# Cross-attention and routed experts: two of the transposes into the row maxima's banks, rank counts behind the output projection, place computation one step later

## The reference, cut to what matters

```python
x = x + tanh(g_xattn[0]) * xattn(layernorm(x), ctx, Wq, Wk, Wv, Wo, bo)   # 8 blocks of 512 rows, 512 wide
x = x + tanh(g_ffn[0])   * ffn(layernorm(x), gate_w, Wu, Wv, Wo)          # each row goes to 2 of 8 experts

def xattn(x, context):                      # 8 heads of 64
    q, k, v = x @ Wq, context @ Wk, context @ Wv
    attn = softmax(q @ k.T / 8)             # per head, 512 x 512
    return (attn @ v) @ Wo + bo

def ffn(x):
    logits = x @ gate_w
    w = softmax(top_k(logits, 2))
    return sum of the two chosen experts' (silu(x @ Wu_e) * (x @ Wv_e)) @ Wo_e, weighted by w
```

## Time and profile before

| | |
|---|---|
| median of 3 runs | 1075.7 us (1075.69 to 1076.78) |
| the profiled execution | 1087.6 us |
| its span on the core | 1085.8 us |
| PE busy in the span | 897.2 us (83%) |
| DVE, ACT, POOL busy | 677.4, 571.8, 538.8 us |

### The profile page before, as it was taken

The page is one execution under the profiler, slowest core; times in us unless marked ns, Lnnn a source line. Parts: engine busy times, 40 slices in busy tenths (PEclk is TensorE's granted clock), DMA queues, the critical chain, the costliest instruction groups (busy, mean ns, idle before and its releaser), DMA issues.

```text
span 1085.8 us, 22768 instructions
## 1 busy us (share of the span) xinstructions
PE 897.2 (83%) x8210; PEld 544.0 (50%) x8210; DVE 677.4 (62%) x1595; ACT 571.8 (53%) x1022; POOL 538.8 (50%) x645
## 2 busy tenths in 40 slices
PE   4878988998899898899899989987540999799880
PEld 2334544555455455455455545544320787577660
DVE  5587876677777766867767786685334454344440
ACT  3366756566557555655755655556120564455450
POOL 6222253343565366546446645547563246556564
PEclk9998999999999999999999999999765899899995
DMA  7447634645633443364354225644343589889996
GB/s 266 132 135 243 215 117 119 170 113 112 191 100 73 133 127 103 75 176 112 75 154 141 68 62 188 185 119 125 110 140 113 142 186 196 167 177 205 189 154 85
DMA packets 125998, 154.53 MB, mean 142 GB/s; under 512 B 48448, under 2 KB 81216, under 8 KB 125120
## 3 DMA queue, kind: packets, MB, share of 16 engines
q1 hardware_dynamic: 102112, 103.08, 33.8%
q0 software_dynamic: 16864, 37.40, 17.8%
q10 hardware_dynamic: 6912, 12.59, 3.8%
HBM read 67.06 MB, written 56.56 MB: 114 GB/s over the span
## 4 chain that ended last, share of the span: by engine, by line
PE 54%; DMA 12%; DVE 12%; issue 8%; ACT 8%; POOL 3%; SPq 1%; POOLq 1%; ACTq 0%; DVEq 0%
PE G L1256 28%; DMA out_dram<-V,Ph 10%; PE ST L1312 4%; PE ST L1313 4%; PE MX L1298 4%; PE G L1265 3%; PE MX L1480 2%; PE PV L1327 2%; PE PV L1329 2%; PE PV L1325 2%; POOL out_dram L670 2%; DVE mx L896 2%; DVE tiles L886 2%; ACT V L853 1%; ACT Ph L705 1%
## 5 line engine op out<-in xcount | busy, mean ns | idle before, releaser
L627 POOL TENSOR_TENSOR Pl<-P,Ph 128x512 f16<-128x512 f32 x128 | 152.3, 1193 | 233.0 <-ACT Ph L705 232.6
L702 ACT ACTIVATE P<-ST 128x512 f32<-128x512 f32 x256 | 153.4, 599 | 195.1 <-PE ST L1313 155.7
L896 DVE TENSOR_REDUCE mx<-MX 128x1 f32<-128x512 f32 x256 | 168.1, 684 | 26.7 <-PE MX L1298 26.7
L705 ACT ACTIVATE Ph<-ST 128x512 f16<-128x512 f32 x256 | 154.8, 605 | 0.4
L670 POOL DMA_INDIRECT out_dram<-V,Ph x78 | 122.2, 1567 | 45.6 <-ACT V L853 30.1
L1480 PE MATMUL MX<-heads,tiles 128*128 128x256 f16 x936 | 119.1, 279 | 17.7 <-DVE heads L1210 17.3
L1325 PE MATMUL PV<-V,Ph 128*128 128x65 f16 x1024 | 113.4, 194 | 12.6 <-issue 12.6
L1327 PE MATMUL PV<-V,Ph 128*128 128x64 f16 x1024 | 113.7, 196 | 1.3 <-issue 1.3
L1329 PE MATMUL PV<-V,Pl 128*128 128x65 f16 x1024 | 113.3, 194 | 1.4 <-issue 1.4
L1325 PEld LDWEIGHTS PV<-V,Ph 128*128 128x128 f16 x1024 | 96.9, 97 | 32.9 <-issue 15.0
L1480 PEld LDWEIGHTS MX<-heads,tiles 128*128 x936 | 91.1, 100 | 39.6 <-issue 22.3
(11 more groups left out here) (206 smaller groups left out, 1877.0 us busy)
## 6 DMA issues: line engine op xcount, KB each, us to landing
heads<-expert_rows SPq DMA_DIRECT2D x39, 516.0 KB
second_norm<-in_x_dram SPq DMA_DIRECT2D x32, 256.0 KB
out_dram<-second_norm SPq DMA_DIRECT2D x32, 256.0 KB
heads<-q_hi SPq DMA_DIRECT2D x124, 64.0 KB
heads<-k_hi SPq DMA_DIRECT2D x124, 64.0 KB
tiles<-in_x_dram ACTq DMA_DIRECT2D x24, 256.0 KB, 3.0
tiles<-in_ctx_dram ACTq DMA_DIRECT2D x24, 256.0 KB, 3.6
expert_rows<-zero_rows SPq DMA_DIRECT2D x8, 516.0 KB, 5.4
```

The source lines that it names most:

```text
L627: nc.gpsimd.tensor_tensor(Pl[:, hh, c, :], P32[:, c, :], Ph[:, hh, c, :], ALU.subtract).then_inc(pl_pool, 1)
L702: nc.scalar.activation(P32[:, c, :], ST[:, c % 2, :], ACT.Exp, scale=0.125 / SC2).then_inc(p_ready, 1)
L705: nc.scalar.activation(Ph[:, hh, c, :], ST[:, c % 2, :], ACT.Exp, scale=0.125 / SC2).then_inc(ph_ready, 1)
L896: nc.vector.tensor_reduce(out=mx[:, k // TT, k % TT:k % TT + 1], in_=MX[:, (k + odd) % 2, :], axis=AXX, op=ALU.max).then_inc(mx_taken, 1)
```

## The change

1. **Places in the banks.** A new function `bank_places` gives each use its bank. The oT transposes of steps up to 31 go into MX (bank g % 2, free once all eight maxima of the step are taken), and so do the transposes of the even context tiles of blocks 1 on (MX bank 1 - g % 2, free once the max rows are copied out). The other uses alternate in G, each waiting for the second one before it in that shorter list. The first two maxima's score tiles of the next step wait for the low parts of what stood in their bank.
2. **PE's order.** Scores of chunk 5 and the max transpose come ahead of the oT transposes; scores of chunk 7 ahead of the output projection; ranks behind the output projection and the second head's last quarters. In the third step the last head's quarter 0 comes ahead of the q projection, and q waits there only for the x tiles, k for the c tiles (before: q for everything).
3. **ACT's order.** The high part of oT comes behind the exponentials of chunk 5 instead of ahead of them.
4. **DVE's order.** `take_ranks` comes behind `x2_rows` and `head_out`; `places` moves into the third step, behind chunk 4's low probabilities; `outsiders` with it.
5. **POOL's order.** The scatter's first half moves to the end of the third step, the second half stays in the fourth.

```diff
@@ bank_uses
         names += first
+        if b:
+            names.append(("out", g - 4))
         if j == 1 and b >= 2:
             names.append(("ranks", b - 2))
-        if b:
-            names.append(("out", g - 4))
         names += second
+def bank_places(uses, TT):
+    steps = 4 * (1 + max(n for kind, n in uses if kind == "v") // TT)
+    places, general = {}, []
+    for kind, n in uses:
+        g = n + 4 if kind == "oT" else 4 * (n // TT - 1) + n % TT // 2
+        if kind == "oT" and g < steps:
+            places[kind, n] = "MX", g % 2, g
+        elif kind == "c" and n >= TT and n % 2 == 0:
+            places[kind, n] = "MX", 1 - g % 2, g
+        else:
+            places[kind, n] = "G", len(general) % 2, general[-2] if len(general) > 1 else None
+            general.append((kind, n))
+    return places
@@ gpsimd step
                     if hh == 0:
...
-                        if g >= 10 and j >= 2:
-                            scatter(b - 2, j - 2)
+                        if b >= 2 and j == 3:
+                            scatter(b - 2, 1)
...
+                if b >= 2 and j == 2:
+                    scatter(b - 2, 0)
@@ scalar step
-                if b:
-                    hi_part(("oT", g - 4), oT[0][:], 1.0)
                 if b == 0:
                     piece_hi(3 * j + 1)
                 exps(hd + 1, 1, 1)
+                if b:
+                    hi_part(("oT", g - 4), oT[0][:], 1.0)
@@ vector step
-                if b:
+                if b == 0:
+                    probs_lo(hd + 1, 1, 0)
+                    piece_lo(3 * j + 1)
+                else:
                     lo_part(("oT", g - 4), oT[1][:], oT[0][:], 1.0)
-                probs_lo(hd + 1, 1, 0)
-                if b == 0:
-                    piece_lo(3 * j + 1)
+                    probs_lo(hd + 1, 1, 0)
+                if j == 2 and b >= 2:
+                    places(b - 2)
+                if g == 10:
+                    outsiders()
...
                 probs_lo(hd + 1, 1, 1)
-                if j == 1 and b >= 2:
-                    take_ranks(b - 2)
                 if b:
                     x2_rows(g - 4)
                 head_out(hd, b % 2)
+                if j == 1 and b >= 2:
+                    take_ranks(b - 2)
...
-                if j == 1 and b >= 2:
-                    places(b - 2)
-                if g == 9:
-                    outsiders()
@@ tensor: bank
-                u = use[name]
-                since(pe, evacuated, u - 1)
-                return G[:, u % 2, :]
+                kind, k, since_ = place_of[name]
+                if kind == "G":
+                    if since_:
+                        pe.wait_ge(evacuated, use[since_] + 1)
+                    return G[:, k, :]
+                if name[0] == "oT":
+                    pe.wait_ge(mx_taken, min(since_ + 2, STEPS) * 2 * TT)
+                else:
+                    pe.wait_ge(mrow_ready, since_ + 2)
+                return MX[:, k, :]
@@ tensor: row_max_scores
+                b, j = divmod(g - 2, 4)
+                if k == 0 and b >= 1:
+                    pe.wait_ge(evacuated, use["oT", g - 6] + 1)
+                if k == 1 and g >= 2 and b < B - 1 and j < 2:
+                    pe.wait_ge(evacuated, use["c", TT * (b + 1) + 2 * j] + 1)
@@ tensor step
                     if proj and k % 2 == 0:
+                        if j == 2 and k == 0:
+                            last_head(0)
                         dst = bank((n, g))
-                        if j == 2 and k == 0:
-                            pe.wait_ge(evacuated, use[n, g])
+                        if j == 2:
+                            pe.wait_ge(evacuated, use["x" if n == "q" else "c", TT * (b + 2) - 1] + 1)
...
+                scores(b, j, 5)
+                if g < STEPS - 1:
+                    max_transpose(g + 1)
                 if b:
                     pe.wait_ge(o_ready, b * HB)
                     transposes(("oT", g - 4), O[(b - 1) % 2][:, j, :])
-                if g < STEPS - 1:
-                    max_transpose(g + 1)
-                scores(b, j, 5)
...
-                if j == 1 and b >= 2:
-                    ranks(b - 2)
+                scores(b, j, 7)
                 if g == 4:
                     pe.wait_ge(w_ready, 4)
                 if b:
                     out_project(g - 4)
-                scores(b, j, 7)
                 weighted(hd, 2)
                 weighted(hd, 3)
+                if j == 1 and b >= 2:
+                    ranks(b - 2)
```

9 lines of the change are left out of this document (6 added, 3 removed).

## The result

| | before | changed |
|---|---|---|
| median, same chip (6 runs each) | 1078.6 us (1075.7 to 1083.7) | 1066.2 us (1062.6 to 1071.3) |
| ratio | | 0.9885, 95% interval 0.9845 to 0.9924 |
| the profiled execution, its span | 1087.6, 1085.8 us | 1071.3, 1069.5 us |

The change makes the kernel 1.15% faster, about 12 us. The forecast was 23.7 us, so 1052 us with a range from 1039 to 1063; 1066.2 lies outside it. A second series on another chip gave the same: 1064.3 against 1079.0 us, ratio 0.9873 (0.9840 to 0.9907).

The account below looks back on a forecast made before the run. PE, busy 83% of the span, was taken as the bound, losing time to waits mostly for DVE. Gains 18.0 (blocks 2 to 6) + 3.9 + 0.6 + 1.2 = 23.7 us, against a median of 1075.7, gave 1052 us, range 1039 to 1063.

Parts of the forecast that it names:

- terms of the first and second step: Blocks 2 to 6: first step gains 0.7 us, second 2.9, together 3.6 a block, after new waits of 0.9 and 1.0.
- The step that failed: First step, projection's end to q: 3.22 us bound by DVE, taken as unchanged; second step's `x2_rows` 0.21 after projection likewise.
- DVE without idle time in the second: Listed sign that the forecast is wrong: DVE never idle in the second step, where it idled 2.16 us before.
- rival 1: DVE becomes the bound in the second step, both new waits 1 us longer: 1063 us, chance 0.12.
- Third and fourth step, "no term": No gain or loss counted: `places` (some 2.5 us) goes under DVE's idle time at the third step's output projection.
- rival 3: Blocks 2 to 6: fourth step's second norm waits for the later scatter half in the row ring: 1082 us, chance 0.03.
- Block 7: Gains 1.2 us: 0.3 in the first step, 0.9 at the end, where the residual's DMA comes earlier.
- POOL's Pl is late in the fourth step: Listed sign that the forecast is wrong: POOL's low probabilities come late in the fourth step.
- rival 4: Granted clock falls once in each first and second step, 1.7 us each, 20 us back: 1072 us, chance 0.05.
- Rival 5: `evacuated` is one count, so x's wait also waits for oT's low part; old waits stay: 1075.7 us, chance 0.03.
- The routing part: Second step, `places` moved away: 0.5 us gained at the maxima's scores, and q no longer waits.
- Blocks 0, 1 and 2: Gains of 0.6 us in block 0, 3.9 in block 1 (0.8 of it clock), 3.6 in block 2.

Follow-up runs that it names:

- experiment 14: Changed kernel with POOL's second-head low probabilities cut to 8 of 512 columns in the first two steps from block 1 on: 1051.2 us, ratio 0.9738 to the kernel before.
- experiment 2: Changed kernel with POOL's two indirect DMAs (rows of no expert, blocks 3 to 6) issued behind its last low probabilities: 1058.0 us, ratio 0.9719 to the kernel before.
- experiment 1: Changed kernel with PE's scores of chunk 7 behind the output projection again: 1055.3 us, ratio 0.9676 to the kernel before.
- experiment 9: Changed kernel with ACT's part undone, oT's high part ahead of chunk 5's exponentials again: 1053.2 us, ratio 0.9773 to the kernel before.
- experiment 4: Changed kernel with DVE's last low probabilities of a step moved ahead of the tiles' low parts, from block 1 on: 1059.1 us, ratio 0.9710 to the kernel before.
- experiment 13: The kernel before, unchanged, profiled again on another chip: span 1073.8 us, median 1078.1 us.
- experiment 12: Changed kernel with ranks, their copy, places and scatter as in the kernel before: 1069.6 us, ratio 0.9903 to the kernel before.
- experiment 3: Changed kernel with DVE's last low probabilities of each step made from one input (P times zero), from block 1 on: 1068.1 us, ratio 0.9796 to the kernel before.
- experiment 11: Kernel before plus only the bank places and PE's order ahead of O's transposes and the third step's q: 1062.8 us, ratio 0.9858.
- experiment 7: Changed kernel with the no-expert indirect DMAs behind POOL's last Pl and chunk 7's scores early only in the first two steps: 1040.9 us, ratio 0.9656 to the kernel before.

## Why the prediction was half right

- **The banks** (terms of the first and second step). The 0.78 and 2.40 us ahead of the context tile went, the new waits came at 0.86 and 0.95 us (worked out: 0.9 and 1.0), and the first step's q wait at 0.70 (0.9). With the collision taken away (experiment 14) a block of 3 to 6 takes 87.0 us against 91.1 before: 4.1 us, forecast 3.6. Some 0.6 of the 4.1 is luck: two of the four second steps in the profile before hold a fall of the clock (25.3 in place of 24.2 us), which the forecast's profile did not. The steps themselves are longer than forecast by 0.4 and 0.7 us (20.55 and 21.72 against 20.2 and 21.0), and the rest came in the fourth step (-1.3), where the wait ahead of the first step's O stood; it is 1.07 us before and 0.50 with the change, and now counts to the first step.
- **The step that failed** is in the first step's working: "From its end to q lie 526.94 - 521.14 - 2.58 = 3.22 us, bound by DVE (`x2_rows`, head output, x's low part), and DVE's order there is unchanged", and the same assumption in the second step, "DVE starts `x2_rows` ... 0.21 after the projection's end". The order was unchanged, but ACT's part puts oT's low part 1 us later, and all behind it on DVE; the early chunk 7 lets POOL's chunk 3 follow chunk 2 at once. Each move was priced on its own engine only. Together they set DVE's last Pl beside 2.28 us of POOL's, and 3.6 us a block are lost, in the four blocks where POOL's two DMAs hold its chunk 2 back until DVE gets there. 4 x 3.6 = 14.4, against the 12.4 missing in blocks 3 to 6. Why chunk 2's delay makes the difference (experiment 2) is shown only so far: with it DVE stays behind both of POOL's, without it behind one. Undoing any one of the three (experiments 1, 2, 9) takes the first step to 20.9, 20.55 and 20.18.
- The text listed "DVE without idle time in the second" step as a sign of being wrong, and that is what the trace shows; but rival 1 got there by DVE's load, and experiment 4 shows that load isn't it.
- **Third and fourth step, "no term".** Wrong in the third by 0.6 us in blocks 3 to 6 and by 1.9 in block 2 (24.05 against 22.20, where `outsiders` stands too): `places` was put where POOL's Pl run. Its cover, DVE's idle time, was there, but not its usual duration. The fourth was right in blocks 2 to 6: no norm waits for the scatter (rival 3), no late Pl.
- **Block 7** (term 1.2) failed as well. Its end was to gain 0.9 us because the residual's DMA would come earlier. The last wait did get 2.0 us shorter, but POOL's Pl is late in the fourth step, which the text had listed as a sign of being wrong: PE waits 7.09 us for it, and the block as a whole takes 0.1 to 2.0 us longer than before.
- **Clock** (rival 4). The three groups of transposes did not bring it down: the granted clock is 1.00 in experiment 14's second step with the same transposes. It fell to 0.50 behind two waits of 1.14 and 0.95 us with four transposes between them, in two of the four blocks that had these waits (in all four in experiment 9, which has them too), and also in the kernel before (experiment 13). In block 1, where the prediction counted half of a fall of 1.7 us, both profiles of the changed kernel have none. What the Trainium skill's rule on transposes ("TensorE: Matmul & The Clock Gate", Part 4) would have done did not show.
- **Rival 5** (one count holds all up) did not come: no wait on PE names a low part that it doesn't need.
- **The routing part** is worth 2 to 3 us by experiment 12's ratio, which is inside the intervals, and 1.6 in each second step less 0.7 in each third by its steps; the prediction counted 0.5 for the maxima and the vanished q wait.
- **Blocks 0, 1 and 2** gained 8.7 us, forecast 8.1.
- **The base.** The fourth steps in the profile that the prediction used held 1.3 us of gaps that experiment 13's have not. Scaling the gain to the runs' median, as the prediction did, kept that out of the number.

The Trainium skill, "SBUF — State Buffer", section "Who interferes with whom", states the rule: DVE and GpSimd share one pair of ports, held for a whole instruction, by a DVE operation with two SBUF inputs (against a GpSimd one that reads SBUF) or in a 2-port mode. The trace agrees that one instruction waits for the other whole (2.72 and 2.58 us in place of 0.68), and experiment 3, `tensor_scalar` with one input, can be the second case by that page, which lists it among the operations that can enter such a mode. The prediction left the rule out: no row of the kernel before showed it at the places that moved. Elsewhere rows did: 8 of DVE's 128 low probabilities took 0.84 to 1.76 us in that profile, in place of 0.68, so it could have stood there as a rival.

## What to carry to other kernels

Where DVE and POOL both work on SBUF, draw the two queues side by side for the order after the change, with their durations, before costing a wait: an operation of 0.2 us takes 1.2 if it lands beside one of POOL's of 1.16, and one of 0.68 takes 2.7 beside two back to back. When an instruction is moved past a POOL instruction's time on another engine, it is the meeting that is new, not the instruction; the cheapest mend can be POOL's own order (here two DMAs put last, experiment 2). And take each part of a bundle by itself: the banks with a part of PE's order (experiment 11) gave as much as the whole, and the whole with two small moves more (experiment 7) gave 38 us in place of 15.

## What the runs showed of the hardware

- POOL's and DVE's operations on SBUF shut each other out whole: 1.62 us beside one of 1.18, 2.72 beside two of 2.28 in all, where 0.68 is usual; POOL loses as well (2.73 for two in place of 2.28). DVE got in between POOL's two in experiment 2, where the second's input was ready 0.17 or 0.26 us before the first ended, and not in the changed kernel's blocks 3 to 6, where it was 0.49 to 0.71; the cause of this is open.
- Kept out: `TENSOR_TENSOR` with both inputs in SBUF, down to 8 columns (1.01 for 0.17), and `TENSOR_SCALAR` with one input (2.45 for 0.41). Not kept out: `BATCH_NORM_STATS2` on SBUF (0.69 beside POOL), and operations whose first input is a PSUM bank (`second_norm<-G`): counted over the changed kernel's profile, eight and seven of them began beside a 512-column operation of POOL's, and took 0.69 and 0.75 us at most.
- The granted clock fell to 1.2 GHz (0.50 from 538.00 to 540.00) and cost 1.65 us in such a step (24.64 against 22.99 in two pairs of otherwise equal second steps of the changed kernel).
- The same kernel's median differs by 1% from chip to chip (1078 and 1088 us). Five times 1.2 us may be gaps of PE with no releaser as in the first profile; the kernel before itself was not profiled on that chip.
